# A transformer block on one core: the first feed-forward layer on pairs of tiles, in two 4-byte pieces

## What is computed

```python
x = _layernorm(x + _L0_attn_ref(x, ...))   # 16 heads of 16, one key and one value head shared by all
x = _layernorm(x + _L0_ffn_ref(x, W1, b1, W2, b2))
x = _layernorm(x + _L1_attn_ref(x, ...))   # inner norm, decaying scan, gated recurrence over the sequence
x = _layernorm(x + _L1_ffn_ref(x, ...))    # product with 6-bit quantised operands
# x: 16 sequences x 512 positions x 256, float32
def _L0_ffn_ref(x, W1, b1, W2, b2):        # _ternary: weights become -1, 0, 1
    h = jnp.einsum('bsd,fd->bsf', x, _ternary(W1)) + b1      # 256 -> 1024
    h = jax.nn.gelu(h, approximate=False)
    return jnp.einsum('bsf,df->bsd', h, _ternary(W2)) + b2   # 1024 -> 256
```

## Time and profile before

| | us |
|---|---|
| median of 3 runs (lowest, highest) | 1768.9 (1768.15, 1773.33) |
| the profiled execution | 1771.39 |
| its span, first to last instruction | 1769.6 |
| PE, DVE, ACT, POOL busy | 1637.5, 1343.4, 1293.2, 1104.3 |
| mean granted PE clock | 0.966 |

### The profile page before, as it was taken

How to read it: one execution, slowest core, us unless ns; L and a number is a source line. 1 busy time by engine, 2 the same in 40 slices (tenths; PEclk the granted TensorE clock), 3 DMA queues, 4 the chain that set the end, 5 groups by cost and what they waited for, 6 DMA issues and landing times.

```text
span 1769.6 us, 84556 instructions
## 1 busy us (share of the span) xinstructions
PE 1637.5 (93%) x35371; PEld 1189.0 (67%) x35371; DVE 1343.4 (76%) x2605; ACT 1293.2 (73%) x2601; POOL 1104.3 (62%) x3392
## 2 busy tenths in 40 slices
PE   5768999999999999999999999999999999999865
PEld 4535667677777777677777777777777767776643
DVE  5546778888788888888888888888888888887454
ACT  3437777788787888778887778887788877887521
POOL 5002346767677776676777767777677776767732
PEclk8879999999999999999999999999999999999875
DMA  9963334444244433444333444334443344431010
GB/s 239 203 93 54 60 58 62 74 72 69 51 72 73 73 66 58 67 73 72 70 61 62 74 72 69 61 62 74 71 71 61 62 71 71 73 58 32 18 29 20
DMA packets 133765, 125.18 MB, mean 71 GB/s; under 512 B 18965, under 2 KB 130633, under 8 KB 133385
## 3 DMA queue, kind: packets, MB, share of 16 engines
q1 hardware_dynamic: 129184, 119.50, 39.1%
q10 hardware_dynamic: 4200, 0.27, 0.2%
HBM read 33.73 MB, written 18.87 MB: 30 GB/s over the span
## 4 chain that ended last, share of the span: by engine, by line
PE 53%; POOL 15%; ACT 10%; issue 8%; DVE 4%; DMA 4%; SPq 4%; POOLq 0%; DVEq 0%; ACTq 0%
PE value_bank L772 11%; PE gen_bank L910 8%; PE score_banks L750 7%; PE gen_bank L598 6%; PE max_banks L590 6%; PE gate_bank L803 5%; ACT L1130 4%; ACT probs L1130 3%; PE gen_bank L819 3%; PE gate_bank L598 2%; POOL square L1613 2%; POOL rstd L1598 2%; DMA key_pieces<-khalf 2%; POOL diff L1717 2%; POOL hseq L1722 2%
## 5 line engine op out<-in xcount | busy, mean ns | idle before, releaser
L1186 DVE TENSOR_REDUCE nmax<-max_banks 128x2 f32<-128x1024 f32 x512 | 622.5, 1216 | 65.3 <-PE max_banks L592 61.3
L1130 ACT ACTIVATE probs<-score_banks 128x1024 f32<-128x1024 f32 x512 | 525.0, 1025 | 112.3 <-PE score_banks L752 96.3
L772 PE MATMUL value_bank<-probs,vaug 128*32 128x128 f32 x8192 | 327.3, 278 | 1.1 <-issue 1.1
L772 PEld LDWEIGHTS value_bank<-probs,vaug 128*32 128x32 f32 x8192 | 205.5, 110 | 90.6 <-issue 79.7
L590 PE MATMUL max_banks<-kaug,qaug 62*128 62x512 f32 x512 | 238.7, 466 | 24.8 <-DVE nmax L1186 15.7
L750 PE MATMUL score_banks<-qaug,kaug 64*128 64x512 f32 x512 | 237.6, 464 | 12.4 <-ACT probs L1130 7.8
L1717 POOL TENSOR_TENSOR diff<-gates 128x16 f32<-128x16 f32 x472 | 114.2, 242 | 212.3 <-ACT gates L1135 205.1
L592 PE MATMUL max_banks<-kaug,qaug 62*128 62x512 f32 x512 | 239.2, 467 | 0.4 <-issue 0.4
L752 PE MATMUL score_banks<-qaug,kaug 64*128 64x512 f32 x512 | 237.6, 464 | 0.0
L1135 ACT ACTIVATE gates<-gate_bank 128x48 f32<-128x48 f32 x472 | 99.0, 210 | 167.6 <-PE gate_bank L803 167.2
L803 PEld LDWEIGHTS gate_bank<-hseq,ghT 128*32 128x32 f32 x11328 | 159.1, 112 | 81.3 <-POOL hseq L1722 57.4
(11 more groups left out here) (234 smaller groups left out, 3540.6 us busy)
## 6 DMA issues: line engine op xcount, KB each, us to landing
qstage<-qhalf SPq DMA_DIRECT2D x384, 128.0 KB
qstage<-qhalf SPq DMA_DIRECT2D x128, 112.0 KB
xt<-in_L_attn_x SPq DMA_DIRECT2D x64, 128.0 KB
xk<-in_L_attn_x SPq DMA_DIRECT2D x16, 512.0 KB, 8.7
residual<-x2s SPq DMA_DIRECT2D x64, 128.0 KB
x2f<-residual SPq DMA_DIRECT2D x64, 128.0 KB
out<-x SPq DMA_DIRECT2D x64, 128.0 KB
qaug<-nmT SPq DMA_DIRECT2D x256, 8.0 KB, 1.8
```

The costliest lines, as they stand in the source:

```text
L772: last = pe.matmul(value_bank[32 * g:32 * g + 32, :].rearrange("p (k t) -> p k t", k=HG)[:, :, u * BLOCK_POS:(u + 1) * BLOCK_POS], vaug[:, ...
L1130: act.activation(probs[:, beat % 2, :, :], score_banks[:, :, :], ACT.Exp).then_inc(exp_done, 1)
L1186: dve.tensor_reduce(nmax[:, m % 2, at:at + 9:8], max_banks[:, :, :], AX_X, ALU.max, negate=True).then_inc(max_taken, 1)
```

## The change

The first layer works on a pair of tiles. `x1` is split into two halves in the 4-byte format for which `F32R` stands (rounded copy and rest), laid side by side for both tiles of a pair, so that a matmul moves 256 columns. In each tile time half of the 1024 rows of the hidden layer is made for both tiles: 2 banks x 2 blocks x 2 pieces x 2 halves of the contraction, 16 matmuls. Gelu takes 256 columns at a time. The second layer adds half of its sum for both tiles into one 512 wide bank; DVE adds it to `x1b` after the pair's first half and makes `x2r` of both tiles after the second. So the feed-forward work has leads of its own, and all behind it comes two tile times later. The tail no longer has a second layer. All tables have new slots. One more transpose is done in quarters (`ATT`), and the keys are stored and placed from POOL's queue.

```diff
-LEAD = dict(LOAD=4, X=3, Q=2, MAX=1, ATTN=0, FFN=-1, SSM=-2, REC=-6, OUT=-7)
+LEAD = dict(LOAD=4, X=3, Q=2, MAX=1, ATTN=0, FFN=-1, PAIRED=-2, SUM=-3, SSM=-4, REC=-8, OUT=-9)
...
-PE_AT = dict(INPUT=0, F2_0=275, F2_1=280, F2_2=285, F2_3=285, F2_4=286, F2_5=288, F2_6=299, F2_7=302, TURND=279, LAST=322, XT=50, Q=12, OUT=128, OT=65, ATT=73, PROJ=90, TURNX=149, B=160, X1T=217, NM=204, FFN1A=247, FFN1B=249)
-ACT_AT = dict(OT=44, TURND=339, XT=104, Q=29, Q8=253, TURNX=196, ATT=145, X1T=230, GELUA=238, GELUB=239, X1=194, X2=178, X4=496)
+PE_AT = dict(INPUT=-2, F2_0=274, F2_1=275, F2_2=278, F2_3=278, F2_4=296, F2_5=297, F2_6=299, F2_7=304, TURND=309, LAST=336, XT=63, Q=8, OUT=134, OT=69, ATT=87, PROJ=100, TURNX=173, B=213, X1T=221, NM=217, FFN1A=240, FFN1B=247)
+ACT_AT = dict(OT=43, TURND=307, XT=51, Q=41, Q8=239, TURNX=158, ATT=99, X1T=193, GELUA=224, GELUB=236, X1=151, X2=202, X4=455)
...
-    SCORES=(19, 61, 89, 107, 137, 157, 178, 231),
-    PAIR=(18, 55, 87, 102, 140, 202, 236, 250),
-    VALUES=(11, 68, 100, 128, 151, 157, 224, 252),
-    STEP=(15, 51, 72, 93, 135, 156, 166, 229),
-    EXP=(86, 121, 165, 181, 186, 227, 228, 236),
+    SCORES=(14, 61, 99, 113, 154, 185, 216, 230),
+    PAIR=(14, 62, 97, 128, 168, 217, 230, 254),
+    VALUES=(3, 87, 111, 130, 180, 203, 227, 240),
+    STEP=(10, 74, 94, 112, 143, 209, 223, 240),
+    EXP=(49, 97, 121, 132, 142, 168, 179, 210),
...
-    FIRST, END = -LEAD["Q"], TILES - LEAD["FFN"]
+    FIRST, END = -LEAD["Q"], TILES - LEAD["SUM"]
...
+            def first_layer(j, bank):
+
+                p, half = divmod(j, 2)
+                for at in range(2):
+                    f = FT // 2 * half + 2 * bank + at
+                    for piece in range(2):
+                        for k in range(KT):
+                            last = pe.matmul(gen_bank[bank][:, at * 2 * P:(at + 1) * 2 * P], w1T[:, k, f * P:(f + 1) * P],
+                                             x1half[:, p % 2, piece, k, :, :].rearrange("p t s -> p (t s)"),
+                                             start=(piece + k == 0), stop=(piece + k == 2), skip_group_check=True)
+                return last
...
                 for half, name in enumerate(("FFN1A", "FFN1B")):
-                    m = mine(name, "FFN")
+                    m = mine(name, "PAIRED")
                     if m is not None:
                         pe.wait_ge(emptied[half], use(half, name, m))
...
+                        pe.wait_ge(emptied[0], use(0, "X1T", m // 2 * 2 + 1) + 1)
+                        first_layer(m, half).then_inc(filled[half], 1)
...
-                        dve.tensor_copy(x1piece[:, 1, :, :], x1rest[:, :, :]).then_inc(x1_step, 1)
-                        dve.wait_ge(x1_step, 2 * m + 1)
-                        dve.tensor_tensor(x1piece[:, 2, :, :], x1rest[:, :, :], x1piece[:, 1, :, :], ALU.subtract).then_inc(x1_step, 1)
...
+            for r in range(2):
+                store_keys(r)
+                place_keys(r)
+            store_keys(2)
```

## The result

The kernel after takes 1798.1 us (median of 4 runs, 1792.6 to 1805.7) for 1771.1 of the kernel before beside it (1768.2 to 1773.6): ratio 1.016, 95% interval 1.011 to 1.020. It is slower by 27 us where 42 us faster was forecast, and outside the range. The profiled execution took 1805.7 us, the longest of the four, with a span of 1803.6.

What follows compares the result with a forecast made beforehand. PE, 98.4% busy in the middle, was taken to set the full tile. Sum: 1771.4 - 59 (full tiles) - 6 (fill) + 28 (drain with tail) - 5 (setup) = 1729.4, at the median 1727 us; 8 in 10 range 1698 to 1762.

Steps and rivals of the forecast that it cites:

- so I let PE's saving through whole: Full tiles 8 to 63: PE's saving of 1.05 us shortens each tile by as much, 56 x 1.05 = -59 us.
- the second limit: ACT with the score banks, exps plus the way to the next tile's first exp: 21.2 us a tile.
- ACT's relief: A tile's first exp comes 1.7 us earlier: 0.74 gelu, 0.58 last normalisation, 0.39 copy of xd.
- the two stay about even; I price the stall at zero: Second score group: PE arrives 1.8 us earlier, the first exp 1.7 us; no wait priced, 0.5 us kept for the range.
- (c): Rival, chance 0.10: ACT's score loop sets the full tile, PE stalls 1.05 us more at the second scores; 1786 us, slower.
- (d): Rival, chance 0.03: first-layer weight loads on PE don't hide, saving 0.07 for 1.19 us a tile; 1789 us, slower.
- first-layer saving: First layer on PE: 16 matmuls at 117 ns, 1.87 us for 3.06, saving 1.19 us a tile.
- Gelu and sums: Each tile: ACT's gelu as four of 256 columns, -0.74 us; DVE's 512 wide sum out of PSUM, +0.3 us.
- Fill: Early tiles: two more tile times at the early pace, -3.2, and gelu gains, -3; together -6 us (0 to -10).
- tail: After the loop: the second layer that holds the tail's second step for 6.48 us goes, -5.3 us.
- Drain: After the last attention: three tile times (21, 18.5, 18.5 us) for one of 24.6, +33.4 us; +28 with the tail's gain.
- Setup: Start of the kernel: storing and placing the keys moves from SP's queue to POOL's, -5 us (-12 to +5).

Runs made afterwards that it cites:

- b_short: Kernel before without the third bf16 piece of the first layer (32 matmuls a tile for 48): 1774.3 us, ratio 1.001.
- a_short: Kernel after without the second piece of the first layer (8 matmuls of 256 columns a tile for 16): 1806.1 us, ratio 1.019 to the kernel before.
- a_mix1: Kernel after with POOL's four mixing operations a recurrence step cut to one sum: 1758.1 us, ratio 0.994 to the kernel before.
- a_fill_x4: Kernel after, three slots changed: step 0 ahead of query product, second scores behind transposes, maxima and step 1, X4 normalisation behind gelu: 1772.0 us, ratio 1.001 to kernel before.
- a_tanh: Kernel after with tanh for gelu, so that both table loads a tile go: 1743.1 us, ratio 0.983 to the kernel before.
- b_tanh: Kernel before with tanh for gelu, so that both table loads a tile go: 1743.0 us, ratio 0.982.

## Why the prediction was wrong

**The step that failed** is "so I let PE's saving through whole", -59 us for -2.2. It rested on PE busy 98.4% and on "in the middle there is no idle PE to take away; only less PE work helps". b_short refutes this: 1.02 us less PE work a tile, 24.59 us a tile. a_short says the same of the kernel after. A full engine was not the one that set the time. What the runs show in its place: stretch A is set by ACT, where 1.14 us more lengthen it by 0.98, and what A loses comes back in B. Which way sets B stays open: less mixing on POOL shortens it by 0.58 us (a_mix1), the three slots of a_fill_x4 by 0.44. I had the number that spoke against it, ACT's 9.8 us from exp to exp, as a limit on the sum of a tile, not as a stretch of its own in which PE may be late or early; and I priced the seven gaps inside a tile at 1.62 us each, the shortest of them, where their mean is 2.10 (14.72 / 7), so that the second limit came out at 21.2 us, far below the 24.5.

**What the change did on ACT.** I put ACT's relief at 0.74 us of gelu, 0.58 of the X4 normalisation and 0.39 of the copy of xd, 1.7 us; A fell by 1.47. That was right. Wrong was "the two stay about even; I price the stall at zero": at the second scores PE waits 0.48 us, and the wait of 0.60 us at the query product, for the bank of the later gelu group, I did not see at all. The X4 and X2 normalisations had to stand somewhere: they stand in front of the eighth exp now, and in the tile shown the first waits 0.45 us there for POOL. From the seventh exp to the eighth it is 2.80 us for 1.84. The second exp comes 3.11 us behind the first for 1.62. PE waits for the first exp, then makes the second scores, and only then the transposes and step 1, while ACT's list has the copy of the transposed x and that step's tanh ahead of the second exp, waiting 0.92 and 0.40 us for them. Of the rivals (c) comes nearest, PE held at SCORES 1 with the saving gone, at 1786 us; the stall there alone is under the 0.75 us that I had given as its point of decision, and with the second wait it is 1.08. But its mechanism is only half right: a_fill_x4 takes the stall away and gets 0.33 us, so the stall is where the time shows and not the limit.

**PE's own terms.** 16 matmuls start 118 ns apart in the median of 700 to 1300 us and their weight loads of 188 ns hide, so (d) is refuted. The first-layer saving was 0.99 us with the changeover for 1.19.

**Gelu and sums:** a gelu operation of 256 columns takes 0.41 us (40.6 us for 98 in 700 to 1300 us; 0.384 taken), the sum of 512 columns 0.69 us (0.72 taken): right.

**Fill and tail** were right in sign: -11.1 for -6, just past the bound of -10, and -4.7 for -5.3. **Drain** was mis-sized: 22.6, 22.5 and 20.8 us for 21, 18.5 and 18.5, +7 us on the sum. The steps inside a tile follow each other in 1.8 us at best, but from the last step of a tile to the first of the next it is 5.3 and 5.5 us (1673.54 to 1678.87, and 1695.90 to 1701.38), which I had not counted. In these pauses PE makes the first layer, ahead of the next tile's input part and first step (two tiles, then a window over most of the second run):

```profile
1673.40 3.72 PE L819 MATMUL gen_bank<-x1half,w1T 128*128 128x256 f32 x16
...
1695.76 3.78 PE L819 MATMUL gen_bank<-x1half,w1T 128*128 128x256 f32 x16
```
```profile
1695.70:1699.50 3.80, 3.80 (x32) 3.54 (x27) 0.09 (x1) 1.68 (x4) 3.17 (x8) 0.50 0.00 0
```

It takes 3.7 us to the next instruction's start for the 2.07 of a full tile: its matmuls start 213 ns apart for 118, at a granted clock of 0.50, the lower of the two levels (1.2 GHz). In the 16.7 us before, PE was busy 8.5 us. The sum had priced these tiles by the steps alone. The third one has no first layer left and takes 20.8 us. What also holds a tile is POOL, where the mixing of the first step comes late:

```profile
1701.16 1.29 POOL L1680 TENSOR_TENSOR hlo<-hT,hhi 128x512 fp32r<-128x512 f32 x1 [1.73 <-ACT hhi L1123]
1702.40 0.61 POOL L1661 TENSOR_TENSOR xd<-q,qscale 128x256 f32<-128x256 fp8e4 x1
1702.98 0.22 POOL L1740 TENSOR_TENSOR diff<-gates 128x16 f32<-128x16 f32 x1
```

Output work and the rest of gelu stand ahead of it in POOL's list (tanh is over at 1701.6, the mixing starts at 1702.98), so the second tanh comes 3.0 us behind the first. a_mix1 adds that three of POOL's four operations a step are 2.6 to 3.7 us of a tile time. **Setup** was wrong in sign in this profile, by a term that lies 12 us apart between kernels with the same setup code.

**What it comes to.** The fill, drain and tail together cost 25 us of span, and nothing in the full tiles pays for them. Three slots bring back 26 us by the medians (in the profiles 18 us in the full tiles and 13 ahead of the first copy), so much of the loss hangs on the order and not on the first layer; this does not show that a better order than the kernel before's exists.

## What to carry to other kernels

A pipelined loop (one in which each engine works on another tile at the same time) is read from one repeating event to the next on the engine that has least slack, in stretches, and each stretch has its own bound; the busy share of an engine, even at 98%, doesn't name it. Lengthening a way by 1 us tells in one run how much slack it has: here PE's additional time came out by half, and a saving on PE alone brought nothing. The reverse does not hold in full: ACT's came out almost whole, and taking 2.56 us from ACT brought 1.0 us at most, because the next way takes over. After work is taken out, look for the waits that appear on the engine relieved, and fill them with what stands behind them before judging the change; a wait that is gone without the loop getting shorter by as much was not the limit.

## What the runs showed of the hardware

A cast of 128x2048 elements on DVE adds about 1 us to one POOL operation that runs beside it: rstd 1.63 us for 0.57, and, with the cast moved, the mixing's product 1.20 for 0.22. The Trainium skill, page "SBUF — State Buffer", section "Who interferes with whom", says that DVE and GpSimd (POOL here) share a pair of ports, that a cast can take it, and that whoever issues first has it for the whole instruction while the other blocks. Both cases agree with it: the slow operation ends 0.03 and 0.07 us behind the cast. The other direction shows in the kernel after, where DVE's subtraction of 512 columns, which ends in `hlo`, takes 1026 ns on the mean of 700 to 1300 us for 641 before (in each of 24 tiles POOL's `x2s`, 0.73 us, has started 0.25 us before it; in the kernel before it starts ahead of POOL's `qin`, which takes 894 ns):

```profile
L1366 DVE TENSOR_TENSOR hlo<-hT,hhi 128x512 fp32r<-128x512 f32 x25 | 25.7, 1026 | 47.4 <-ACT hhi L1123 47.4
```
```profile
L1361 DVE TENSOR_TENSOR hlo<-hT,hhi 128x512 fp32r<-128x512 f32 x25 | 16.0, 641 | 0.0
```

That the shared ports are the cause of this one was not tried. Tanh needs no table load of its own here: in the rows of ACT above it follows exp without one (770.09), a load stands in front of gelu (770.29), and behind gelu tanh runs at 775.24, before the load for exp at 776.24. ACT loads a table twice a tile, and 1.28 us each is what a_tanh and b_tanh took away.
